# Stacking the first batch's keys in three column parts over the SyncE and GpSimd queues, with a buffer for each context chunk and another order of the first maxima pieces

## What is computed

```
Q = heads(layernorm(x) @ Wq);  K = heads(ctx @ Wk);  V = heads(ctx @ Wv)
attn = softmax(Q @ K.T / 4);   x = x + (attn @ V) @ Wo + bo
x = x + fp4_feed_forward(layernorm(x))
```

## Time and profile before

| what | value |
|---|---|
| median of three runs | 3254.37 us |
| the profiled execution | 3257.17 us |
| its span, first to last instruction | 3255.3 us |
| mean granted TensorE clock | 0.976 of 2.4 GHz |
| TensorE busy | 3155.6 us, 97% |
| VectorE busy | 2671.2 us, 82% |
| first piece matmul starts at | 36.51 us |
| first score matmul starts at | 84.27 us |

### The profile page before, as it was taken

The page is one execution under the profiler, slowest core; times in us unless marked ns, Lnnn a source line. Parts: engine busy times, 40 slices in busy tenths (PEclk is TensorE's granted clock), DMA queues, the critical chain, the costliest instruction groups (busy, mean ns, idle before and its releaser), DMA issues.

```text
span 3255.3 us, 55791 instructions
## 1 busy us (share of the span) xinstructions
PE 3155.6 (97%) x19606; PEld 1664.1 (51%) x19606; DVE 2671.2 (82%) x6006; ACT 2265.5 (70%) x4692; POOL 1099.6 (34%) x1414
## 2 busy tenths in 40 slices
PE   6989999999999999999999999999999999999997
PEld 4444555545445455555545455455555545455445
DVE  5878888888898888888888897888889888887865
ACT  1667767777776777777777776777777777776762
POOL 0213333333333333333333333333333343333333
PEclk6889999999999999999999999999999999999998
DMA  3422323332332322232232232322233231232200
GB/s 71 77 44 49 55 44 65 47 57 37 58 58 38 67 44 49 50 58 54 45 61 38 52 58 38 67 48 48 46 61 55 41 67 32 52 58 39 46 19 10
DMA packets 121103, 163.29 MB, mean 50 GB/s; under 512 B 47445, under 2 KB 93926, under 8 KB 120826
## 3 DMA queue, kind: packets, MB, share of 16 engines
q1 hardware_dynamic: 120506, 159.12, 27.9%
q10 hardware_dynamic: 320, 0.62, 0.2%
HBM read 46.22 MB, written 8.39 MB: 17 GB/s over the span
## 4 chain that ended last, share of the span: by engine, by line
PE 88%; DVE 6%; ACT 3%; issue 1%; POOL 1%; ACTq 0%; DMA 0%; SPq 0%; DVEq 0%; POOLq 0%
PE out_ps L1065 23%; PE ring L1052 17%; PE ring L1085 16%; PE ring L1015 8%; PE ring L1026 5%; PE ring L982 4%; DVE piece_max L1434 4%; PE ring L990 4%; ACT probs L1205 2%; PE ring L1006 2%; PE ring L971 2%; PE ring L966 2%; PE ring L1023 2%; PE ring L1000 1%; PE ring L1010 1%
## 5 line engine op out<-in xcount | busy, mean ns | idle before, releaser
L1434 DVE TENSOR_REDUCE piece_max<-ring 128x1 f32<-128x402 f32 x4096 | 2059.6, 568 | 347.6 <-PE ring L1085 335.0
L1205 ACT ACTIVATE probs<-ring 128x512 f32<-128x512 f32 (+1 forms) x3328 | 1760.6, 607 | 502.1 <-PE ring L1052 496.3
L1065 PE MATMUL out_ps<-probs,v_ones 128*17 128x512 f32 x6656 | 890.8, 607 | 1.0 <-ACT probs L1205 0.9
L1085 PE MATMUL ring<-k_stack,q_stack 48*128 48x402 f32 x4096 | 828.5, 391 | 23.1 <-issue 8.9
L1052 PE MATMUL ring<-q_stack,k_stack 50*128 50x512 f32 (+1 forms) x3328 | 829.2, 457 | 9.1 <-issue 2.9
L1052 PEld LDWEIGHTS ring<-q_stack,k_stack 50*128 50x128 f32 (+1 forms) x3328 | 357.2, 182 | 707.6 <-issue 278.8
L1085 PEld LDWEIGHTS ring<-k_stack,q_stack 48*128 48x128 f32 x4096 | 455.5, 189 | 326.7 <-DVE piece_max L1434 123.6
L1015 PE MATMUL ring<-wgu_T,xq_T 128*128 128x512 f32 (+1 forms) x1080 | 264.1, 389 | 1.9 <-POOL xq_T L1539 0.6
L1493 POOL TENSOR_SCALAR h<-h 128x704 f32<-128x704 f32 x60 | 46.7, 778 | 626.3 <-DVE h_small L1245 626.3
L1015 PEld LDWEIGHTS ring<-wgu_T,xq_T 128*128 128x128 f32 x1080 | 191.8, 188 | 56.3 <-issue 26.9
L1065 PEld LDWEIGHTS out_ps<-probs,v_ones 128*17 128x17 f32 x6656 | 110.6, 95 | 210.1 <-issue 151.3
(11 more groups left out here) (170 smaller groups left out, 2638.5 us busy)
## 6 DMA issues: line engine op xcount, KB each, us to landing
k_stack<-k_parts SPq DMA_DIRECT2D x252, 200.1 KB, 4.3
k_stack<-k_parts SPq DMA_DIRECT2D x252, 100.1 KB, 4.3
ctx_in<-in_ctx SPq DMA_DIRECT2D x47, 384.0 KB, 4.1
q_stack<-q_parts SPq DMA_DIRECT2D x256, 64.0 KB, 2.3
x_in<-in_x SPq DMA_DIRECT2D x16, 512.0 KB, 5.6
q_stack<-q_parts SPq DMA_DIRECT2D x256, 32.0 KB, 2.0
resid<-in_x SPq DMA_DIRECT2D x62, 128.0 KB, 2.7
out<-x SPq DMA_DIRECT2D x62, 128.0 KB, 1.7
```

The source lines that it names most:

```text
L1065: last = pe.matmul(out_ps[32 * j:32 * j + V1, :], v_ones[0:r, batch % 2, m, PER_GROUP * g + j, :], probs[0:r, prob_slot(batch, step, j), : ...
L1085: pe.matmul(ring[:, bank(kind, batch, item), 0:PW], q_stack[rows, at, t * P:(t + 1) * P], k_stack[rows, at, a:b], start=True, stop=True).t ...
L1205: act.activation(probs[0:r, prob_slot(batch, step, j), :], ring[0:r, at, :], ACT.Exp, scale=SCORE_SCALE).then_inc(probs_ready, 1)
L1434: dve.tensor_reduce(piece_max[:, g % 2, 2 * u + half, t, c:c + 1], ring[:, at, 0:PW], AX_X, ALU.max).then_inc(pieces_max, 1)
```

## The change

`LEAD_IN` is written out as one list for the whole prologue, in which `pieces` entries say after which event how many pieces follow; the spreading is gone. In it:

- SP's first loads go out without waits in the order context 0, Wk, x, context 1, Wq, context 2, Wv, context 3, Wo: chunks 2 and 3 load into `wd_T`, which is not yet in use, and each chunk has a semaphore of its own.
- The key projection of chunk 1 moves behind the transposes of chunks 2 (second half) and 3 (first half).
- The first keys are stacked in three column parts (512, 512 and 577 columns), each once its own chunk's low part is there. ACT issues none of them. GpSimd issues, in this order: pair 1 part 0, pair 0 part 0, queries of pair 0, pair 1 part 2 (16 DMAs). SP issues: queries of pair 1, pair 1 part 1, pair 0 part 1, pair 0 part 2 (16 DMAs).
- The pieces go by (c, u) in the order of `FIRST_PIECES`, and each group of eight waits for the parts that it reads. The first eight stand ahead of the bias and of all value projections, the value staging ahead of them.
- Of the four DMAs of the finished maxima ACT issues two.

```
+    ('k_proj', 0, 0), ('ln1_apply',), ('ctx_T', 1, 0), ('stack_k', 1, 0), ('ctx_T', 1, 1), ('x_T', 0), ('x_T', 1),
+    ('ctx_T', 2, 0), ('ones',), ('q_proj', 0), ('ctx_T', 2, 1), ('stack_k', 0, 0), ('stack_q', 0), ('ctx_T', 3, 0),
+    ('k_proj', 0, 1), ('ctx_T', 3, 1), ('k_proj', 0, 2), ('stack_q', 1), ('k_proj', 0, 3), ('prep_v',), ('pieces', 8),
+    ('stack_k', 1, 1), ('stack_k', 0, 1), ('bias',), ('v_proj', 0), ('pieces', 4), ('stack_k', 0, 2), ('stack_k', 1, 2),
+    ('pieces', 4), ('v_proj', 1), ('pieces', 4), ('stack', 1, 0), ('v_proj', 2), ('pieces', 8), ('v_proj', 3),
+    ('pieces', 8), ('pieces', 4), ('v_proj', 4), ('pieces', 8), ('v_proj', 5), ('pieces', 8), ('pieces', 8), ('v_proj', 6),
...
+FIRST_QUEUE = {('stack_q', 0): 'pool', ('stack_q', 1): 'sp', ('stack_k', 0, 0): 'pool', ('stack_k', 1, 0): 'pool', ('stack_k', 0, 1): 'sp', ('stack_k', 1, 1): 'sp', ('stack_k', 0, 2): 'sp', ('stack_k', 1, 2): 'pool'}
+FIRST_PIECES = [(0, 0), (0, 1), (1, 0), (2, 0), (1, 1), (3, 0), (2, 1), (3, 1)]
...
-            return early_ctx if kind == "start" and c % 2 else ctx_in[:]
+            return [ctx_in[:], early_ctx, wd_T[:, 0:4, :], wd_T[:, 4:FT, :]][c] if kind == "start" else ctx_in[:]
...
+        def stack_first(eng, event):
+            u = event[1]
+            if event[0] == "stack_q":
+                first_split_done(eng, ("q_proj", 0))
+                stack_queries(eng, 0, 0, u, first_queries[u])
+            else:
+                part = event[2]
+                first_split_done(eng, ("k_proj", 0, part))
+                if part == 2:
+                    first_split_done(eng, ("k_proj", 0, CHUNKS - 1))
+                stack_keys(eng, 0, 0, u, part * NQ, NK if part == 2 else (part + 1) * NQ, first_keys[u][part])
...
-                    if u == t == c == half == 0:
-                        pe.wait_ge(first_queries, STACKED)
-                    if t == c == half == 0:
-                        pe.wait_ge(first_keys[u], STACKED // 2)
-                    elif t == half == 0 and c == PIECES - 1:
-                        pe.wait_ge(stacked[at], stacked_until(u))
+                    if t == half == 0:
+                        if n // (2 * QT) == [v for _, v in FIRST_PIECES].index(u):
+                            pe.wait_ge(first_queries[u], STACKED // 2)
+                        for part in range(min(c, 2) + 1):
+                            pe.wait_ge(first_keys[u][part], STACKED // 2)
...
+                    if kind == "start":
+                        act.wait_ge(*drained(kind, batch, event))
+                        first_shift(act, (1,))
```

More of the change, by code:

```diff
@@ L118 @@
 RINGS, RING_FOR = (7,), (0, 0, 0, 0)
[L121 to L126, removed]
+LEAD_IN = [
+    ('load_ctx', 0),
+    ('load_k',),
+    ('load_x',),
+    ('load_ctx', 1),
+    ('load_q',),
+    ('load_ctx', 2),
+    ('ctx_T', 0, 0),
+    ('load_v',),
+    ('load_ctx', 3),
+    ('ctx_T', 0, 1),
+    ('prep_k',),
+    ('load_o',),
+    ('ln1_stats',),
+    ('k_proj', 0, 0),
+    ('ln1_apply',),
+    ('ctx_T', 1, 0),
+    ('stack_k', 1, 0),
+    ('ctx_T', 1, 1),
+    ('x_T', 0),
+    ('x_T', 1),
+    ('ctx_T', 2, 0),
+    ('ones',),
+    ('q_proj', 0),
+    ('ctx_T', 2, 1),
+    ('stack_k', 0, 0),
+    ('stack_q', 0),
+    ('ctx_T', 3, 0),
+    ('k_proj', 0, 1),
+    ('ctx_T', 3, 1),
+    ('k_proj', 0, 2),
+    ('stack_q', 1),
+    ('k_proj', 0, 3),
+    ('prep_v',),
+    ('pieces', 8),
+    ('stack_k', 1, 1),
+    ('stack_k', 0, 1),
+    ('bias',),
+    ('v_proj', 0),
+    ('pieces', 4),
+    ('stack_k', 0, 2),
+    ('stack_k', 1, 2),
+    ('pieces', 4),
+    ('v_proj', 1),
+    ('pieces', 4),
+    ('stack', 1, 0),
+    ('v_proj', 2),
+    ('pieces', 8),
+    ('v_proj', 3),
+    ('pieces', 8),
+    ('pieces', 4),
+    ('v_proj', 4),
+    ('pieces', 8),
+    ('v_proj', 5),
+    ('pieces', 8),
+    ('pieces', 8),
+    ('v_proj', 6),
+]
+FIRST_QUEUE = {('stack_q', 0): 'pool', ('stack_q', 1): 'sp', ('stack_k', 0, 0): 'pool', ('stack_k', 1, 0): 'pool', ('stack_k', 0, 1): 'sp', ('stack_k', 1, 1): 'sp', ('stack_k', 0, 2): 'sp', ('stack_k', 1, 2): 'pool'}
+FIRST_PIECES = [(0, 0), (0, 1), (1, 0), (2, 0), (1, 1), (3, 0), (2, 1), (3, 1)]
 VECTOR_ROUNDS = [3]
@@ L332, in put_rounds @@
                         put(cost, "round", e, i)
[L334 to L345, removed]
         if kind == "start":
+            first = 0
             for e in PROLOGUE:
[L349 to L353, removed]
+                if e[0] == "pieces":
+                    for n in range(first, first + e[1]):
+                        put(0, "piece", PHASES, n)
+                    first += e[1]
+                else:
+                    put(0, "event", e)
+                    put_rounds([e])
+            assert first == NPIECE
             put(0, "event", ("max_parts", 0))
@@ L1212, in body @@
                 for what, *item in SEQUENCE[kind]:
-                    if what == "round" and item[1] == len(round_parts(item[0])) - 1 or what == "event" and item[0][0] in ("prep_k", "prep_v", "stack_k"):
+                    if what == "round" and item[1] == len(round_parts(item[0])) - 1 or what == "event" and item[0][0] in ("prep_k", "prep_v", "stack_q", "stack_k"):
                         handle(kind, batch, item[0])
```

101 lines of the change are left out of this document (57 added, 44 removed).

## The result

The changed kernel takes 3236.3 us (median of 6 runs, 3226.02 to 3239.16) against 3254.32 for the kernel before (6 runs, 3251.34 to 3256.78): a ratio of 0.9946, 95% interval 0.9934 to 0.9957, or 18.0 us less. The forecast was 11.5 us less. The profiled execution took 3238.56 us with a span of 3236.8 (before: 3257.17 and 3255.3).

What follows compares the result with a forecast made beforehand. The prediction took TensorE as busy 97% of the span, with a prologue hole behind ACT's DMA queue. An earlier last reduction (-10.2 us) and the maxima (-1.3) sum to -11.5, so 3254.37 becomes 3243 us, range 3236 to 3252.

Steps and rivals of the forecast that it cites:

- the forecast case: Prologue: GpSimd issues at about 1.1 us per DMA, first score near 72.8 us, time 3243 us; chance 0.44.
- rival 1: Prologue: GpSimd issues cheaply at 0.57 us (3238), or TensorE's clock stays at 2.4 GHz (3237); chance 0.18.
- The first piece: Prologue: GpSimd's twelve DMAs at 1.1 us each from 14.2, plus 2.3 landing, put the first pieces at 29.7 us.
- First piece to last reduction: Prologue pieces and values: 38.68 us before, adjusted to 38.8; last reduction at 68.5 instead of 78.72, -10.2 us.
- TensorE at 1.2 GHz stays the longer: Stretch of first pieces: VectorE needs 64 x 0.50 = 32 us, so TensorE at the low clock sets its 38.8.
- Maxima: End of prologue: two queues issue two maxima DMAs each, -1.3 us, with 0 as the other end.
- Sum: Prologue gain of -11.5 us, reaching the end whole: median 3254.37 to 3242.9 us.
- It just comes in time, and I cost it at nothing: Part 1 of pair 0's keys: there at 35.5 to 38.3 us, wanted at 39.7; cost nothing.
- rival 2: Second key part: SP's eight issues choke, TensorE waits 4 us there; 3247 us, chance 0.16.
- Loads: Lead-in: chunks 2 and 3 load earlier, but no wait on them is on the path; cost nothing.
- ACT's freeing: Prologue: without ACT's eight DMAs value staging runs in the lead-in, and the hole from 36.5 to 40.0 us goes.
- Rivals 3 and 4: GpSimd's issues: dear at 1.5 to 2.6 us, 3248 to 3261, chance 0.15; or starved by VectorE, 3265, chance 0.07.

Runs made afterwards that it cites:

- experiment 1: Kernel before the change, with ACT's eight first-key DMAs issued by GpSimd and nothing else changed; 3255.86 us, ratio 1.0007 to the kernel before.
- experiment 11: Changed kernel with the old mix: two pieces ahead, then four or five behind each half round of values; 3238.75 us, ratio 0.9956 to the unchanged kernel.
- experiment 10: Changed kernel with all first stacking and maxima DMAs on SP, two context buffers, pieces pair by pair; 3239.77 us, ratio 0.9955 to the unchanged kernel.
- experiment 4: Changed kernel with the two old context buffers and their waits for chunks 2 and 3; 3233.85 us, ratio 0.9935 to the unchanged kernel.
- after: The changed kernel, against the kernel without the change; 3236.3 us, ratio 0.9946.
- experiment 6: Changed kernel with ACT in GpSimd's place for the first stacking DMAs; 3240.06 us, ratio 0.9967 to the unchanged kernel.
- before: The kernel without the change; 3254.32 us.
- experiment 9: Changed kernel with four pieces behind each half of a round of values, instead of between whole rounds; 3233.86 us, ratio 0.9934 to the unchanged kernel.
- experiment 7: Changed kernel with all four maxima DMAs issued by SP; 3235.33 us, ratio 0.9943 to the unchanged kernel.

## Why the prediction was right, and where it was not

Faster by over 0.2%: right. The time lies 0.3 us inside the low end of the range, so that the range held is in part luck, and what came was not the forecast case but one half of rival 1: GpSimd was cheap. The clock, its other half, rose for some 7 us, but the stretch was shorter mainly for a reason that no case had. By the forecast's own steps:

- **The first piece: 26.25, not 29.7.** The step that failed is "I take 1.1 us, midway between 0.59, an unhindered issue of SP, and 1.61, ACT's median key issue". GpSimd's issue costs 0.52 to 0.53 in the median, a little below SP's. Of the two rows ACT's was the wrong neighbour: experiment 1 shows that those long issues came with a jam of transfers, which was not there at 14 to 24 us, and not with the engine. The Trainium skill's 1 us for GpSimd's first byte (DMA: Bandwidth & Descriptors, Specifications) is no price of an issue; by it the first piece would have been at 28.5. The four query DMAs took 0.51 to 0.53 us to issue and 2.8 to 3.4 from issue to landing. Rival 1's own sum, 24.5, was 1.8 too early: the queries' low part came at 21.09 instead of 19.8, and the last query DMA took 3.35 us from its issue.
- **First piece to last reduction: 35.9 us, not 38.8.** The step that failed is "Before: 38.68 us for 62 pieces and all values", carried over to another order of the same work. It held 0.30 us a matmul, and in that 2.8 us of waits for ACT's copies of the values. Experiment 11, with the old mix of work, took 39.5, so the term was right for the kernel that I read it from; with whole rounds of values it fell to 35.9, at 0.25 us a matmul and the same 0.50. "TensorE at 1.2 GHz stays the longer" was wrong too, as the clock was at the 2.4 GHz level for some 7 us, but there VectorE held the pieces up, and an estimate gives the rise 0.3 us. In rival 1 I priced only a clock that never falls.
- **Maxima: -0.25 us, not -1.3.** "ACT is idle there" was true and beside the point: its two issues took 1.1 us each, so the queue that ended last was hardly sooner. The range's other end, 0, was nearer.
- **Sum.** -3.45 - 2.9 + 1.05 = -5.3 us, and the first score came at 67.47 where 72.8 was forecast. Behind the first score the profiled run gained another 1.8 us. There the granted clock differs between the two executions (from 250 to 300 us 0.93 before and 1.00 after), and no experiment tells whether the change has a part in that.
- **"It just comes in time, and I cost it at nothing"** (the second part of the keys): right, with more to spare than forecast. SP's eight issues of part 1 ran at 0.57 to 0.60 us from 24.53, and TensorE waited for no part. So rival 2 fell; but its wait of 2.1 us appears in experiment 10, where SP sends everything and pair 0 goes first.
- **Loads**: "no wait on their loads is on the path, so I cost this at nothing" missed 1.3 us (experiment 4): no wait, but a slower landing of the queries. **ACT's freeing**: the bias followed the pieces as forecast, but experiment 1 corrects the reading behind it, "what stands in the hole: ACT's own queue". ACT's queue stood there, and without it the hole was no shorter: the step that a chain of waits names is not always the one to remove.
- **Rivals 3 and 4** fell. GpSimd issued at 0.51 to 0.56 us, with VectorE at work beside it or not. The Trainium skill's rule (SBUF — State Buffer, Who interferes with whom) on GpSimd's descriptors kept waiting by VectorE did not decide here; whether VectorE's other modes would hold GpSimd up, no run here shows.

What the change consists of, then, by the marks: of the 18.1 us from split to score 11.5 are the first piece, 5.9 us behind the split instead of 17.4; 6.3 are the stretch from it to the last reduction, 35.9 us instead of 42.2; 0.3 the maxima. Of the 6.3, experiment 11 leaves 2.7, the hole behind the first two pieces, and 3.6 come with the new list. With the queue, the buffers, the order and the split of the maxima undone 11.3 of the 18.1 remain (experiment 10): that is sending each part as soon as its chunk is split and starting on it, the new list, and ACT's freedom together. The four are worth 6.8 together and 2.3 singly, in part because they cover for each other and in part because the single marks hold different stretches of the clock.

## What to carry to other kernels

When a queue's issues are long, look at what they land before blaming the issuer: a jam of transfers is cured by sending earlier in smaller parts, and moving the same DMAs to an idle engine leaves it as it is. Put DMAs on an engine that has nothing urgent behind them: ACT was the dear place here because of the copies behind it, while SP and GpSimd could not be told apart by the time. A length read from one order of work holds for that order; what waits are in it has to be looked up before it is carried over. Parts of a change that can each be undone almost for nothing may still carry it together, so undo them together before dropping any; and compare runs from the last mark that they have alike.

## What the runs showed of the hardware that was not expected

- GpSimd's DMA issue, 0.53 us in the median (0.51 to 0.76), is no dearer than SP's 0.59; 16 of them in after and eight in experiment 1 (0.50 to 0.76) agree. ACT's were 1.1 each for two maxima DMAs in after, and in experiment 6 0.73 to 2.28 for its first four keys but 0.58 to 0.77 for the next eight.
- The clock came back to the 2.4 GHz level before the last reduction in all eleven kernels with new lists of pieces, and stayed at 0.50 in the three with the old mix (before, 1 and 11). What decides it stays open. In after TensorE was busy 11.75 of 11.80 us at 0.50 from 26.2 to 38, then came 1.00; in experiment 11 it was busy 3.85 to 4.00 us of every 4 from 26 to 62 and nothing came. Grouping by whole rounds is not it (experiment 9).
- A busy share near 1 does not say that TensorE works at one pace: at the same 0.50 its matmuls came every 0.25 us in after, 0.28 in experiment 9 and 0.30 in 11.
- The granted clock reads 1.00 from the start to 22 us, but durations say otherwise: five of the 512-column key projections took 2.47 us at 9.44 and 1.41 at 20.05 in after. "At the full 2.4 GHz" in the prediction read that column alone. The lead-in also differs between executions: the query split starts at 20.40 in after, where the eight transposes of x ahead of it took 1.97 us, and at 19.05 in experiment 7, where they took 1.09, with the same prologue up to there. So 1.3 us of a mark in the prologue can be chance, as with the split of after against that of before.
